# A two-layer transformer kernel: when the experts' rows are loaded for the final sums, into how many buffers, and how many tiles TensorE sums

## The reference, cut to what matters

```python
xn = layernorm(x)
x = x + attention(xn) + moe(xn)          # attention over the 4 sequences at the same position

def moe(x):                              # T = 2048 tokens
    topk_idx, topk_w = route(x)          # 8 of 64 experts for each token
    w_full = zeros(T, 64).at[arange(T)[:, None], topk_idx].add(topk_w)
    for wg, wu, wd, we in experts:       # 64 experts, 256 -> 176 -> 256
        out += (silu(x @ wg.T) * (x @ wu.T)) @ wd.T * we[:, None]
```

## Time and profile before

| | us |
|---|---|
| median of 3 runs | 1179.88 (1179.0 to 1183.53) |
| the profiled execution's own time | 1184.52 |
| its span, first to last instruction | 1182.7 |
| TensorE busy | 1087.1 (92%) |
| VectorE busy | 704.8 (60%) |
| ScalarE busy | 655.8 (55%) |
| GpSimd busy | 459.1 (39%) |

### The profile page before, as it was taken

One profiled execution on the slowest core, in us unless ns is written; L12 is line 12 of the kernel. 1 busy time (PEld: TensorE's weight loads), 2 busy tenths in 40 slices (PEclk: granted clock), 3 DMA queues, 4 the chain that ended last, 5 costly groups with the idle time before them and its releaser, 6 DMA issues. The chain is left out here.

```text
span 1182.7 us, 25082 instructions
## 1 busy us (share of the span) xinstructions
PE 1087.1 (92%) x7605; PEld 667.5 (56%) x7606; DVE 704.8 (60%) x2445; ACT 655.8 (55%) x1340; POOL 459.1 (39%) x525
## 2 busy tenths in 40 slices
PE   6679999999999999998879669999999999999985
PEld 3345666666666656663655425555555555555564
DVE  6486656656656666661228836566565656566566
ACT  4214455555555544446243738777877787787720
POOL 4323231322222000000330047777677777777510
PEclk9799999999999999999899979999999999999997
DMA  7500131113111310101110675484557646676277
GB/s 237 98 9 12 30 52 30 31 31 51 31 30 31 48 25 22 22 2 56 36 36 6 166 172 177 142 264 152 179 169 236 191 137 201 189 228 228 76 267 284
DMA packets 81681, 129.65 MB, mean 110 GB/s; under 512 B 32777, under 2 KB 53002, under 8 KB 81035
## 3 DMA queue, kind: packets, MB, share of 16 engines
q1 hardware_dynamic: 61576, 76.94, 23.3%
q0 software_dynamic: 15360, 47.21, 13.0%
q10 hardware_dynamic: 4616, 3.91, 1.2%
HBM read 97.57 MB, written 30.05 MB: 108 GB/s over the span
## 5 line engine op out<-in xcount | busy, mean ns | idle before, releaser
L684 DVE CUSTOM_DVE_ANT_0 a_masked<-a_ps_s,a_mask 128x512 bf16<-128x512 f32 (+3 forms) x512 | 229.9, 487 | 160.4 <-PE a_ps_s L843 156.6
L600 ACT ACTIVATE a_probs<-a_ps_e 128x512 f32<-128x512 f32 (+1 forms) x384 | 188.3, 527 | 122.6 <-PE a_ps_e L863 121.6
L1854 PE MATMUL e_ps_gu<-e_w_gu,e_xT 128*64 x640 | 208.6, 469 | 1.1 <-DVE e_xT L1724 1.1
L189 POOL DMA_INDIRECT yn<-rows,inv x160 | 162.1, 1013 | 122.3 <-DVE inv L1404 60.5
L1854 PE MATMUL e_ps_gu<-e_s_gu,e_xT 128*64 128x352 f32 x640 | 208.6, 469 | 0.0
L1633 POOL DMA_INDIRECT y<-e_y,dst x160 | 161.3, 1008 | 60.5 <-issue 28.9
L1879 PE MATMUL e_ps_y<-e_w_d,e_hT 88*64 x640 | 151.4, 379 | 0.9 <-DVE e_hT L1749 0.9
L1879 PE MATMUL e_ps_y<-e_s_d,e_hT 88*64 88x256 f32 x640 | 151.4, 379 | 0.0
L843 PE MATMUL a_ps_s<-a_kT,a_qT 72*128 72x512 bf16 (+3 forms) x512 | 131.3, 301 | 13.9 <-DVE a_headmax L684 11.1
L860 PE MATMUL a_ps_e<-a_qT,a_kT 75*128 75x512 bf16 (+3 forms) x512 | 140.8, 303 | 2.1 <-ACT a_probs L600 1.8
L1854 PEld LDWEIGHTS e_ps_gu<-e_w_gu,e_xT 128*64 128x64 f32 x640 | 81.7, 137 | 90.6 <-issue 90.6
(11 more groups left out here) (243 smaller groups left out, 1888.6 us busy)
## 6 DMA issues: line engine op xcount, KB each, us to landing
e_w_gu<-e_gu SPq DMA_DIRECT2D x64, 352.0 KB
e_w_d<-e_down SPq DMA_DIRECT2D x64, 176.0 KB
a_qT<-qk_parts SPq DMA_DIRECT2D x48, 192.0 KB
e_w_gu<-y SPq DMA_DIRECT2D x12, 768.0 KB, 6.6
qk_parts<-a_stage SPq DMA_DIRECT2D x16, 256.0 KB, 2.6
e_w_gu<-y SPq DMA_DIRECT2D x4, 1024.0 KB, 7.8
qkv<-y SPq DMA_DIRECT2D x12, 256.0 KB
yn<-rows,inv POOLq DMA_INDIRECT x160, 3.7
```

What stands on the lines that cost most here:

```text
L189: eng.indirect_dma_start(self.x[:, j % self.NS, :], None, t["rows"], bass.IndirectOffsetOnAxis(inv[:, j:j + 1], 0)).then_inc(self.x_in[j % ...
L600: nc.scalar.activation(probs[:, i % HKV, UCOL[u]:UCOL[u + 1]], ps_e[:, (i * 3 + u) % 2, 0:w], ACT.Exp, scale=SCALE0).then_inc(exp_done, 1)
L684: ins = V.tensor_tensor_reduce(masked[:, n % 2, c:c + w], ps_s[:, n % 2, c:c + w], mask[:, T - w:T], 1.0, -3e38, ALU.add, ALU.max, headmax ...
L1854: ins = nc.tensor.matmul(ps_gu[r * SEG:(r + 1) * SEG, j % 2, 0:2 * INTER1], xT[:, j // 2 % 2, j % 2, k * P + r * SEG:k * P + (r + 1) * SEG ...
```

## The change

SP no longer waits for all 160 scatters but for those of the blocks with rows: VectorE works out at block 100, for each of the 8 semaphores, how many of these blocks it counts (`filled`), from `last`, the block in which the last expert ends. The rows go into 8 buffers: 5 in slots 0 to 14 of `w_gu` and 3 in slots 0 to 14 of `w_d`; slot 15, which the blocks without rows still read, is left alone. Their landing is counted on the weight loads' 8 semaphores, and the early rows have one of their own. TensorE sums six tiles (1, 4, 7, 10, 12, 14) and VectorE ten.

```diff
-        LEAD, BEHIND, NF = 2, 4, 5
+        LEAD, BEHIND, NF = 2, 4, ring.FIRST
+        turns = sbuf(ctx, nc, "e_turns", [1, SCATTERS])
-        y8 = w_gu[:, :, :, :].rearrange("p s k i -> p (s k i)")[:, 0:NF * TOPK * D].rearrange("p (f c) -> p f c", f=NF)
+        spare_gu = w_gu[:, 0:NW - 1].rearrange("p s k i -> p (s k i)")
+        spare_d = w_d[:, 0:NW - 1].rearrange("p s k d -> p (s k d)")
+        y8 = [spare[:, f * TOPK * D:(f + 1) * TOPK * D] for spare, n in ((spare_gu, 5), (spare_d, 3)) for f in range(n)]
+        filled = seg_expert[0:1, 3 * P - 1 - NY:3 * P - 1]
-            return y8_in[i % NF], (i // NF + 1) * 16 + (0 if i % NF else EARLY_COUNT)
-        ON_DVE = [i for i in range(NT) if i % 3 != 2]
+            return w_in[i % NF], NE // ring.FIRST * 32 + (i // NF + 1) * 16
+        ON_PE = (1, 4, 7, 10, 12, 14)
+        ON_DVE = [i for i in range(NT) if i not in ON_PE]
...
+            counts = [sp.value_load(filled[0:1, b:b + 1], min_val=16, max_val=NBLK // NY * 16) for b in range(NY)]
             for b in range(NY):
-                sp.wait_ge(y_out[b], NBLK // NY * 16)
+                sp.wait_ge(y_out[b], counts[b])
             for i in range(NT):
                 f = i % NF
                 if i >= NF:
                     sp.wait_ge(*done_of(i - NF))
                 n = LATER if i in EARLY_TILES else TOPK
-                sp.dma_start(y8[:, f, 0:n * D]..., rows8[i, :, 0:n, :]).then_inc(y8_in[f], 16)
+                sp.dma_start(y8[f][:, 0:n * D]..., rows8[i, :, 0:n, :]).then_inc(w_in[f], 16)
...
+                    ch.step(V.tensor_tensor(turns[:, :], last[0:1, NE - 1:NE].to_broadcast([1, NY]), iota[0:1, 0:NY],
+                                            ALU.subtract))
+                    ch.step(V.tensor_scalar(turns[:, :], turns[:, :], (NY - 1) / 2, 1.0 / NY, ALU.add, ALU.mult))
+                    ch.step(V.tensor_scalar(turns[:, :], turns[:, :], 2.0 ** 23, None, ALU.add))
+                    ch.step(V.tensor_scalar(filled, turns[:, :], -2.0 ** 23, 16.0, ALU.add, ALU.mult))
...
-            pe.wait_ge(early_in, EARLY_COUNT + 16)
-            for i in range(2, NT, 3):
+            pe.wait_ge(early_in, EARLY_COUNT)
+            for n, i in enumerate(ON_PE):
```

More of the change, by code:

```diff
@@ L1529, in layer1_experts @@
             ctx, nc, "e_summed", "e_o_added", "e_x_done_a", "e_x_done_b", "e_stored")
-        y8_in = sems(ctx, nc, *(f"e_y8_in{f}" for f in range(NF)))
-        early_in, EARLY_COUNT = y8_in[0], 32 + len(EARLY_TILES) * 16
+        early_in, = sems(ctx, nc, "e_early_in")
+        EARLY_COUNT = 32 + len(EARLY_TILES) * 16
         def landed_y8(i):
-            return y8_in[i % NF], (i // NF + 1) * 16 + (0 if i % NF else EARLY_COUNT)
-        ON_DVE = [i for i in range(NT) if i % 3 != 2]
+            return w_in[i % NF], NE // ring.FIRST * 32 + (i // NF + 1) * 16
+        ON_PE = (1, 4, 7, 10, 12, 14)
+        ON_DVE = [i for i in range(NT) if i not in ON_PE]
         def done_of(i):
-            return (x_done_b, i // 3 + 1) if i % 3 == 2 else (x_done_a, i - (i + 1) // 3 + 1)
+            return (x_done_b, ON_PE.index(i) + 1) if i in ON_PE else (x_done_a, ON_DVE.index(i) + 1)
         def add_up(eng, E, i, ch, done):
@@ L1547, in fold @@
             def fold(n, other):
-                ch.step(E.tensor_tensor(y8[:, f, 0:n * D], y8[:, f, 0:n * D], other, ALU.add))
+                ch.step(E.tensor_tensor(y8[f][:, 0:n * D], y8[f][:, 0:n * D], other, ALU.add))
             if i in EARLY_TILES:
                 fold(EARLY_ROWS, early8[:, i, :])
-                fold(LATER - 4, y8[:, f, 4 * D:LATER * D])
+                fold(LATER - 4, y8[f][:, 4 * D:LATER * D])
             else:
-                fold(4, y8[:, f, 4 * D:8 * D])
-            fold(2, y8[:, f, 2 * D:4 * D])
-            fold(1, y8[:, f, D:2 * D])
+                fold(4, y8[f][:, 4 * D:8 * D])
+            fold(2, y8[f][:, 2 * D:4 * D])
+            fold(1, y8[f][:, D:2 * D])
             eng.wait_ge(o_added, ON_DVE.index(i) + 1)
-            E.tensor_tensor(x_sb[:, i, :], x_sb[:, i, :], y8[:, f, 0:D], ALU.add).then_inc(done, 1)
+            E.tensor_tensor(x_sb[:, i, :], x_sb[:, i, :], y8[f][:, 0:D], ALU.add).then_inc(done, 1)
         def gate_up_copied(j):
@@ L1615, in _ @@
                 n = LATER if i in EARLY_TILES else TOPK
-                sp.dma_start(y8[:, f, 0:n * D].rearrange("p (k d) -> p k d", d=D), rows8[i, :, 0:n, :])\
-                  .then_inc(y8_in[f], 16)
+                sp.dma_start(y8[f][:, 0:n * D].rearrange("p (k d) -> p k d", d=D), rows8[i, :, 0:n, :])\
+                  .then_inc(w_in[f], 16)
         @block.gpsimd
@@ L1820, in _ @@
                     ch.step(V.tensor_scalar(scattered, bound[:, :], 1.0 - 2.0 ** 23, 16.0, ALU.add, ALU.mult))
+                    ch.step(V.tensor_tensor(turns[:, :], last[0:1, NE - 1:NE].to_broadcast([1, NY]), iota[0:1, 0:NY],
[3 more added lines that the diff above has]
+                    ch.step(V.tensor_scalar(filled, turns[:, :], -2.0 ** 23, 16.0, ALU.add, ALU.mult))
             for q in range(len(ON_DVE)):
                 add_attention(q)
-            dve.wait_ge(early_in, EARLY_COUNT + 16)
+            dve.wait_ge(early_in, EARLY_COUNT)
             for i in range(NT):
-                if i % 3 != 2:
+                if i in ON_DVE:
                     add_up(dve, V, i, ch, x_done_a)
                 else:
-                    dve.wait_ge(summed, i // 3 + 1)
-                    V.tensor_tensor(x_sb[:, i, :], x_sb[:, i, :], ps_gu[:, i // 3 % 2, 0:D], ALU.add)\
+                    n = ON_PE.index(i)
+                    dve.wait_ge(summed, n + 1)
+                    V.tensor_tensor(x_sb[:, i, :], x_sb[:, i, :], ps_gu[:, n % 2, 0:D], ALU.add)\
                      .then_inc(x_done_b, 1)
@@ L1906, in _ @@
                 oldest, now = now, after
-            order = ON_DVE + list(range(2, NT, 3))
+            order = ON_DVE + list(ON_PE)
             def turn_y(q):
@@ L1931, in _ @@
                 output(q, ps_out[q % 2][:, 0:D], True)
-            pe.wait_ge(early_in, EARLY_COUNT + 16)
-            for i in range(2, NT, 3):
+            pe.wait_ge(early_in, EARLY_COUNT)
+            for n, i in enumerate(ON_PE):
                 f = i % NF
-                q = len(ON_DVE) + i // 3
+                q = len(ON_DVE) + n
                 if q + 1 < NT:
                     turn_y(q + 1)
-                if i // 3 >= 2:
-                    pe.wait_ge(x_done_b, i // 3 - 1)
-                output(q, ps_gu[:, i // 3 % 2, 0:D], False)
+                if n >= 2:
+                    pe.wait_ge(x_done_b, n - 1)
+                output(q, ps_gu[:, n % 2, 0:D], False)
                 pe.wait_ge(*landed_y8(i))
                 for k in range(TOPK):
-                    row = y8[:, f, k * D:(k + 1) * D]
+                    row = y8[f][:, k * D:(k + 1) * D]
                     if i in EARLY_TILES and k >= LATER:
                         row = early8[:, i, (k - LATER) * D:(k - LATER + 1) * D]
-                    ins = nc.tensor.matmul(ps_gu[:, i // 3 % 2, 0:D], ident[:, :], row,
+                    ins = nc.tensor.matmul(ps_gu[:, n % 2, 0:D], ident[:, :], row,
                                            start=False, stop=(k == TOPK - 1))
```

## The result

The changed kernel takes 1172.23 us (median of 6 runs, 1168.57 to 1177.61) against 1181.92 for the kernel before in the same runs: a ratio of 0.9921, 95% interval 0.9898 to 0.9944. The forecast was 1170.0, that is 9.9 us less than before; 9.7 us less was measured. The kernel before came out at 1181.92 and not at the 1179.88 that the forecast started from; that is 2.0 of the 2.2 us by which 1172.23 lies above it. The profiled execution took 1177.61 us, and its span is 1175.8.

The account below looks back on a forecast made before the run. The end was taken as bound by buffers and the sharing of tiles. 1.1 (product fewer) + 2.6 (tile handed over) + 7.0 (waits gone) - 1.0 (new wait), rest rounding, made 9.9 us off 1179.88: 1170.0, range 1166 to 1176.

Parts of the forecast that it names:

- Which scatters are waited for: SP's first load of rows follows the scatter of block 153, not 159, by 2.49 us: 13.4 us earlier.
- Loads beside the last blocks: Eight row loads during the last six expert blocks land by 1135.3 and slow TensorE by zero, 1 us allowed.
- The four operations at block 100: Four more VectorE operations at block 100, 0.7 us, hidden by TensorE: taken as 0.
- The start of VectorE's folds: With one attention product fewer to add, VectorE's sums start at 1138.43 instead of 1139.52.
- VectorE's list: VectorE's sums at the end: 7 early tiles, 3 full and 6 of TensorE's take 31.1 us, 2.6 less.
- Does TensorE keep up?: TensorE's six sums in the end: VectorE waits only at tile 1, 1.0 us; 1.7 us to spare at the last.
- Do the loads keep up?: Row loads 8 to 15 in the end have 6.8 us or more each, tile 10 tightest: no wait taken.
- The sum: VectorE's last addition in the end comes at 1170.5 plus 0.1 instead of 1180.53: 9.9 us earlier.
- the second rival: At the end, the early release brings nothing, first load still at 1130: up to 1.5 us later, 1171.5; chance 0.06.
- late rows: In the end, rows of tile 10, 12 or 14 land late and TensorE stands: costs 3.5 to 5 us, 1174; chance 0.12.
- the low clock: In the end, TensorE at 1.2 GHz after late rows becomes the bound: two such tiles give 1183.6; chance 0.05.
- The chances: Whole kernel against before: faster (below 1174.0) 0.87, same 0.09, slower 0.04.

Follow-up runs that it names:

- f6_seven_tiles: Changed kernel with TensorE summing seven tiles instead of six: time from first attention product to VectorE's last addition 44.6 us against 43.7, ratio to the kernel before 0.994.
- e2_no_release: Changed kernel with its old wait for all 160 scatters: time from first attention product to VectorE's last addition 45.0 us against 43.7, ratio to the kernel before 0.9958.
- e4_five_buffers: Changed kernel with five buffers instead of eight: time from first attention product to VectorE's last addition 53.6 us against 43.7, ratio to the kernel before 0.9993.
- e1_buffers_only: Kernel before with eight buffers alone, old scatter wait and five TensorE tiles: first attention product to VectorE's last addition 46.2 us against 53.4, ratio 0.9956.

## Why the prediction was right, step by step

- **Which scatters are waited for**: right. 2.48 us from the scatter of block 153 to the first load, as forecast (2.49).
- **Loads beside the last blocks**: nothing lost, as taken: 13.05 us from the scatter of block 153 to the first product, with the loads and without. They were through about 1140, or 1137 in the forecast's time, where it said 1135.3. The last of the eight, tile 7's, is not needed before TensorE's sum at 1150.79, so the 2 us cost nothing.
- **The four operations at block 100**: hidden, as taken. From the scatter of block 99 to that of block 153 it is 137.47 us before and 137.48 after.
- **The start of VectorE's folds**: 1141.17 - 2.74 = 1138.43, to the hundredth.
- **VectorE's list**: 1141.17 to 1173.64 is 32.5 us; forecast 31.1 + 1.0 + 0.1 = 32.2. The wait at tile 1 was 1.14 us instead of 1.0.
- **Does TensorE keep up?** Yes. VectorE took up its last sum 1.3 us after it was done, forecast 1.7. f6_seven_tiles shows how near it is: one tile more and it is the bound.
- **Do the loads keep up?** Nearly, and here a detail was wrong. I took no wait, and called tile 10 the tightest. TensorE waited 1.00 us for the rows of tile 12, whose load went out right behind that of tile 11, a full one: from its issue at 1151.93 it took 9.3 us, and the layout left it 8.4. I had set the time left against the median landing, without counting what was queued ahead of this load. VectorE was more than 1 us behind, so it cost nothing:

```profile
1161.27 2.86 PE L1959 MATMUL e_ps_gu<-e_w_gu,ident_sb 128*128 128x256 f32 x12 [1.00 <-DMA e_w_gu<-y]
```

- **The sum**: 9.9 us forecast, 9.6 in the end, 9.7 in the median. The parts of the forecast, 1.1 + 2.6 + 7.0 - 1.0, make 9.7, and with the wait as measured, 1.14, they make 9.6. What was called rounding is that the list gives 0.3 us less than the trace before too (33.8 + 7.0 against 41.0), and the forecast set a counted list against a measured one. The share of each edit was near as well: buffers 7.1 us (forecast: waits of 7.0), the sixth tile 2.5 (2.6 + 1.1 - 1.0 = 2.7), the release nothing alone and 1.3 with the others (at most 1.5). The size of this last is right, its place is not: the second rival had tile 7's rows in time and tile 15's late, while e2_no_release has TensorE waiting for tiles 7 and 10, and tile 15 waits for nothing.
- **The rivals**: late rows did not decide here. That of the low clock is real: e4_five_buffers shows its every step, and as forecast two such tiles are enough to give back the whole gain. Two of its numbers are off. It put the slower sum at about 2 us, but 6.11 us stand against 3.46 for a sum alone, so 2.7 us, as e4_five_buffers has it (6.27 against 3.62); with the waits alone the two late loads would have ended at 1178.3 and not at 1179.4. And it had every late load followed by a slow sum, where waits of 1.96 to 2.48 us were not.
- **The chances**: by its own parts faster would have been 0.89, not 0.87.

## What to carry to other kernels

When an engine waits for a transfer that is issued only when its buffer comes free, more buffers help and an earlier first transfer does not; but as soon as the consumers start earlier, the first transfer's time decides. Here the early release was worth 0 us by itself in one order of work and 11.5 us in another, and the three more buffers 7.1 us in the first and 0.9 in the second. So what such an edit is worth belongs to the order of work around it. Write out the lists of both consumers with start-to-start times from the trace: here this gave the end to 0.3 us, and it also shows the best share between them and the idle slots worth filling. A stall on TensorE must be priced with the slower work that may follow it, and not by its length alone: behind a wait of 5.06 us 16 matmuls took 2.7 us longer, behind one of 2.48 us 12 took no longer.

## What was not expected of the hardware

The end repeats to 0.02 us (43.73 us three times, on two chips at least; 53.36 and, where only what is worth nothing was changed, 53.38 us). So do the blocks on the fast chips: from the first scatter to that of block 153 it is 402.18 to 402.20 us in all seven profiles there, with and without the change. Yet the whole kernel varies by some 9 to 11 us from run to run on one of these chips; in the profiles this difference is all there at the first scatter (706.1 to 714.7 us).

Between chips it varies by 10 to 11% (the kernel before: 1182, 1305 and 1312 us in the median). In e1_buffers_only, on one of the slower chips, the first gather of the experts starts at 679.3 us, much as elsewhere (before: 682.8), but the first product at 1246.4 instead of 1127.2, and the stretch of 402.2 us lasts 524.6; in the other profiles of the slower chips it is 522 to 539. So the 120 us lie in the blocks, whose engines stand there for 3 to 8 us at a time; the chain of waits names "issue" or "another core or an unknown queue" as what ended it. No run tells what it is.
